# Splitting the first two large experts' weights two turns earlier, and finishing the last large expert in quarters, in a two-layer language-model tower on one core

## The chip, the cores and the metric

One NeuronCore of one Trainium2 chip runs the whole program in one launch. The metric is device time in microseconds (us); lower is better.

## The reference, cut to what matters

A token embedding for 32 batches of 128 tokens (width 192), a causal attention, a soft mixture of 64 small experts, a 12-head attention with rotary positions, and last a routed mixture of 8 large experts:

```python
router_logits = xf @ router_w                       # 4096 tokens x 8 experts
expert_gate  = max(softmax(router_logits)); expert_index = argmax(...)
position_in_expert = cumsum(one_hot(expert_index))  # over all tokens, in order
# a token past the expert's capacity of 512 is dropped
h = gelu(einsum('ecd,edm->ecm', expert_inputs, w1) + b1)      # 192 -> 768
expert_outputs = gelu(einsum('ecm,emd->ecd', h, w2) + b2)     # 768 -> 192
out = einsum('ecd,tec->td', expert_outputs, combine)          # gate times output, back to the token
return h_before + out
```

All of it is in float32. For some products a matrix is split into a high part (written as `fp32r`) and a low part (what that left over), and the products of the parts are summed.

## The kernel before, in words

The program is written engine by engine: in each phase a block gives SP (DMA issue), POOL (GpSimd), PE (TensorE), ACT (ScalarE) and DVE (VectorE) its own list of instructions, and semaphores (`wait_ge`, `then_inc`) order them across engines. An engine runs its list strictly in the order in which it is written. Three phases matter here.

**`combine_phase`** combines the small experts' outputs, computes the second attention, adds it to `h`, and routes. It runs as a software pipeline in turns t = 0 to 37 over 32 batches (`NB`). A turn works on several batches at once: `y` (batch t: combine), `q` (t-1: heads and rotary), `a` (t-2: softmax and values), `p` (t-3: projection, layernorm). Routing goes by pairs of batches: `r` (router logits, from turn 5 on, every second turn), `z` (choice of the expert and counting, one turn later), `w` (row of each token in its expert's table, and the scatter by indirect DMA into `routed_inputs`, one more turn later). At the end the turns are thin: turn 32 has a, p, q and z; turn 33 has a, p, r, w; turn 34 p, z; turn 35 r, w; turn 36 only z of the last pair; turn 37 only w of the last pair. PE is given products that nobody reads (`keep_busy`, L67) in its waits there.

DVE's part of the routing is a chain of small operations: L1797 and L1798 (logits less their maximum), L1834 to L1863 (choice, one-hot, running count, `chosen`), PE's counting product (L1637, recorded as L60), L1804 to L1807 (`read_counts`), L1829 to L1853 (row of the token, `placed`), then POOL's two scatters (L1561).

The first two large experts' w1 are loaded in turn 28 (`load_first_weights`). Their high parts are made by ACT (L1774) at the ends of turns 34 and 35, their low parts by DVE (L1945) at the ends of turns 35 and 36. The second expert's parts lie in the buffers of the small experts' outputs, which turn 31 reads last.

When the last pair's scatters have landed, SP and ACT load the rows of large experts 0 and 1, and the block ends. POOL waits for the scatters too.

**`expert_phase`** with `routed_to` set runs the 8 large experts. For expert n PE makes the hidden layer in six pieces of 128 units (m = 0 to 5; five products each, L60), ACT applies the activation (L1319), PE turns the rows of expert n+2 (L1218), and then makes the output: four groups j of 128 rows, six products of 192 columns each (L1246; the profile has 48 records for the 24 products). The groups lie in two PSUM banks, two groups in each, and are signalled by halves. DVE adds the bias (L1404, a half of 384 columns at a time), ACT applies the activation (`send`, L1304), DVE multiplies by the gate (`gate`, L1409 and L1413), and POOL scatters each group of 128 rows with an accumulating indirect DMA into the output (L1197). `send(n-1)` stands on ACT behind the second hidden piece of expert n; `gate(n-1)` stands on DVE before the bias of expert n; for the last expert (n = 7) both follow at the very end. POOL waits for `gated` before groups 0 and 2, and at the end for `stored`, the landing of all scatters.

Of the kernel before, what the change touches and what calls it, by code (L numbers as in the profile page):

```python
# [21 lines left out]
F32 = mybir.dt.float32  # L22
# [1034 lines left out]
def expert_phase(nc, T, name, L, dst, b2, act_fn, sem_of, routed_to=None, then=None):  # L1057
# [9 lines left out]
    with ExitStack() as ctx:  # L1067
# [41 lines left out]

        def ybank(u):  # L1110

            return bank[:, 4 + 2 * u:6 + 2 * u, 0:2 * D]
# [9 lines left out]
        with nc.Block() as block:  # L1122

            @block.sync
            def _(sp):
# [41 lines left out]
                if then is not None:  # L1167
                    then.sync(sp)

# [16 lines left out]
            if routed:  # L1186

                @block.gpsimd
                def _(pool):
                    def turn(i):  # L1190
                        for u in range(2):
                            n = i * 2 + u

                            for j in range(4):
                                if j % 2 == 0:
                                    wait_apart(pool, gated, 2 * n + j // 2 + 1)
                                pool.indirect_dma_start(  # L1197
                                    out=routed_to,
                                    out_offset=bass.IndirectOffsetOnAxis(ap=numbers[u][:, j, :], axis=0),
                                    in_=ysum[u][:, j, :], in_offset=None, bounds_check=NB * P - 1,  # L1200
                                    oob_is_err=False, compute_op=ALU.add).then_inc(stored[u], 16)

                    each_pair(pool, turn)
                    for u in range(2):
                        pool.wait_ge(stored[u], 64 * turns)

            @block.tensor
            def _(pe):
# [13 lines left out]
                def turn(i):  # L1222
                    for u in range(2):
# [16 lines left out]
                        past(pe, y_added, halves * (n - 1))  # L1240
                        for j in range(4):
                            js = slice(j * P, (j + 1) * P)
                            for k in range(MT):
                                if j == 0:
                                    pe.wait_ge(acted, n * MT + k + 1)
                                last = pe.matmul(ybank(u)[:, j // 2, (j % 2) * D:(j % 2 + 1) * D], hf[:, k, js],  # L1246
                                                 w2s[u][:, k, :], start=k == 0, stop=k == MT - 1)
                            if (j + 1) % (4 // halves) == 0:
                                last.then_inc(w2_done, 1)
# [14 lines left out]
            def _(act):  # L1264
# [32 lines left out]
                def send(n, u):  # L1297

                    if routed:

                        past(act, gated, 2 * (n - 1))
                        for k in range(2):
                            act.wait_ge(y_added, 2 * n + k + 1)
                            act.activation(stage[u][:, 2 * k:2 * k + 2, :], ysum[u][:, 2 * k:2 * k + 2, :], act_fn  # L1304
                                           ).then_inc(act_steps, 1)
# [5 lines left out]
                def turn(i):  # L1311
                    for u in range(2):
                        n = i * 2 + u
                        if not isinstance(n, int) or (2 if routed else 1) <= n + 1 < n_exp:
                            w1_hi(n + 1, 1 - u, i + u)
                        for m in range(MT):
# [4 lines left out]
                            if m == (1 if routed else MT - 1) and (not isinstance(n, int) or n > 0):  # L1321
                                send(n - 1, 1 - u)
                        if routed:
                            load_tags(n, u)
# [20 lines left out]
            def _(dve):  # L1345
# [35 lines left out]
                def turn(i):  # L1381
                    for u in range(2):
# [17 lines left out]
                        y_in = ybank(u).rearrange("p a (c d) -> p a c d", c=2)  # L1400
                        for k in range(halves):
# [17 lines left out]
                if routed:  # L1419
                    gate(n_exp - 1, 1, turns - 1)  # L1420
# [4 lines left out]
def combine_phase(nc, ins, T, out, early, large, sem_of):  # L1425
# [3 lines left out]
    with ExitStack() as ctx:  # L1429
# [78 lines left out]
        with nc.Block() as block:  # L1508
# [34 lines left out]
            def _(pool):  # L1543
# [40 lines left out]
                for k in range(3):  # L1584
                    pool.wait_ge(scattered[k], 32 * ((NPAIR + 2 - k) // 3))
# [128 lines left out]
            def _(act):  # L1714
                def exp_combine(b):
# [5 lines left out]
                def turn(t, u, n, y, q, a, p, r, z, w):  # L1721
# [14 lines left out]
                    if z is not None:  # L1736
                        act.wait_ge(S["logits_read"], z + 1)
                        act.activation(lex[:], lx[:], ACT.Exp).then_inc(S["router_exped"], 1)
                    if a is not None:
# [6 lines left out]
                    if q is not None:  # L1746
                        act.wait_ge(S["qkT_done"], q + 1)
                        past(act, S["S_done"], 4 * q)
                        act.activation(kqT[:], bank[:, 1:3, 0:3 * P], ACT.Copy).then_inc(S["qk_took"], 1)  # L1749
                    if y is not None:  # L1750
# [19 lines left out]
                    if t in (NB + 2, NB + 3):  # L1770

                        k = t - NB - 2
                        act.wait_ge(large.w1_in[k], 48)
                        act.activation(large.w1hi[k][:], large.w1raw[k][:], ACT.Copy).then_inc(large.w1_hi_ready, 1)  # L1774

# [9 lines left out]
            def _(dve):  # L1785
# [15 lines left out]
                def read_counts(z):  # L1801
# [6 lines left out]
                                             ).then_inc(S["counts_read"], 1)  # L1808

# [8 lines left out]
                def turn(t, u, n, y, q, a, p, r, z, w):  # L1818
# [102 lines left out]
                    if p is not None:  # L1921
                        dve.wait_ge(steps, stats5)
                        dve.tensor_scalar(ve[:, 1:2], mv[:, 1, 1:2], EPS, None, ALU.add).then_inc(S["ln5_var"], 1)
                    if z is not None:
                        read_counts(z)
# [15 lines left out]
                    if t in (NB + 3, NB + 4):  # L1941
                        k = t - NB - 3

                        dve.wait_ge(large.w1_hi_ready, k + 1)
                        dve.tensor_tensor(large.w1lo[k][:], large.w1raw[k][:], large.w1hi[k][:].bitcast(F32),  # L1945
                                          ALU.subtract).then_inc(large.w1_split, 1)
# [77 lines left out]
```

## Time and profile before

| what | us |
| --- | --- |
| median of 3 runs | 1408.03 |
| range of the runs | 1406.95 to 1409.55 |
| the profiled execution, its own time | 1409.95 |
| its span, first to last instruction | 1408.2 |
| PE busy | 1332.5 (95%) |
| DVE busy | 971.5 (69%) |
| ACT busy | 936.1 (66%) |
| POOL busy | 253.6 (18%) |
| mean granted TensorE clock | 0.986 |

The span is 1.75 us shorter than the execution's own time. The busy shares say which engine is full on average over phases with different limits; what a change in one stage is worth is read from the chain of waits and from the instructions of that stage in order of time. In the routing's last turns and after the last matmul, PE is mostly idle or runs products that nobody reads.

### The profile page before, as it was taken

The page shows a single profiled execution, that of the slowest core. Times are in us where ns is not written, and L with a number is a line of the kernel's source. Part 1 is how long each engine was busy: PE and PEld are TensorE (multiplying, and loading weights), DVE is VectorE, ACT ScalarE, POOL GpSimd, SP SyncE. Part 2 cuts the span into 40 slices and gives each one's busy share as a digit, 9 for nine tenths or more (in the row PEclk, how much of TensorE's full clock was granted, in tenths as well). Part 3 has the DMA queues.
Part 4 walks back from the last instruction along what each step waited for, and adds up shares of the span by engine and source line. Part 5 has one row for each costly group of instructions (what it writes and reads, how often), then busy time and mean ns, then how long its engine had stood idle before and what let it go on. Part 6 is the DMA issues. An engine that isn't in the chain of part 4 may idle for free. (4 is left out here: it accounts for less than half of the span.)

```text
span 1408.2 us, 29711 instructions
## 1 busy us (share of the span) xinstructions
PE 1332.5 (95%) x9086; PEld 1190.7 (85%) x9086; DVE 971.5 (69%) x2953; ACT 936.1 (66%) x2209; POOL 253.6 (18%) x284
## 2 busy tenths in 40 slices
PE   8799999998999999999999999799999999879995
PEld 6688888886899989998999998688898888768895
DVE  7888877555877777777777773588888888632321
ACT  1488888886666666666666664488888888725551
POOL 5422200001111111111111110012122122111344
PEclk9999999999999999999999999999999999989998
DMA  6144444455666666656665664544454547015631
GB/s 199 45 159 162 162 153 154 157 203 170 196 196 197 186 189 190 200 182 198 190 193 185 193 188 160 160 150 140 154 160 139 152 149 215 15 48 147 158 70 17
DMA packets 181635, 221.04 MB, mean 157 GB/s; under 512 B 25348, under 2 KB 148458, under 8 KB 181536
## 3 DMA queue, kind: packets, MB, share of 16 engines
q1 hardware_dynamic: 147904, 179.52, 41.0%
q10 hardware_dynamic: 25952, 33.32, 7.2%
q0 software_dynamic: 7680, 6.95, 2.7%
q8 instruction: 52, 0.85, 0.3%
q14 instruction: 47, 0.39, 0.1%
HBM read 142.36 MB, written 79.90 MB: 158 GB/s over the span
## 5 line engine op out<-in xcount | busy, mean ns | idle before, releaser
L1246 PE MATMUL bank<-e_w,e_h_full 128*128 128x192 f32 x1920 | 324.7, 326 | 0.4
L1246 PEld LDWEIGHTS bank<-e_w,e_h_full 128*128 128x128 f32 x1920 | 310.6, 190 | 1.7 <-ACT e_h_full L1319 1.3
L1319 ACT ACTIVATE e_h_full<-bank,e_b 128x512 f32<-128x512 f32 x240 | 165.2, 689 | 191.5 <-PE bank L60 191.5
L1180 POOL TENSOR_TENSOR e_ln_rstd<-e_ln_var_eps,minus_half 128x4 f32<-128x4 f32 x62 | 62.5, 1008 | 450.6 <-DVE e_ln_var_eps L1369 450.6
L1727 ACT ACTIVATE probs<-bank,head_neg_max 128x128 f32<-128x128 f32 x384 | 134.9, 393 | 7.6 <-DVE head_neg_max L1823 5.7
L1376 DVE TENSOR_SCALAR e_rows<-e_slot_sums,e_ln_mean_var,e_ln_rstd 128x192 f32<-128x192 f32 x248 | 77.5, 376 | 77.6 <-POOL e_ln_rstd L1180 77.6
L1289 ACT ACTIVATE e_x_full<-bank,e_ln_shift,e_ln_gain 128x512 f32<-128x512 f32 x124 | 89.7, 774 | 44.8 <-PE bank L1218 44.8
L1002 PE MATMUL bank<-x,dispatch_weights 128*128 128x193 f32 x512 | 95.7, 329 | 6.9 <-ACT slot_stage L845 5.9
L60 PE MATMUL bank<-e_x_hi,e_w1hi 128*128 128x512 f32 x216 | 95.4, 442 | 2.3 <-ACT e_h_full L1319 1.2
L1607 PE MATMUL bank<-slot_outputs_then_w_part,combineT 128*128 128x193 f32 x512 | 94.0, 336 | 2.5 <-ACT combineT L1719 2.1
L1404 DVE TENSOR_TENSOR e_stage<-bank,e_b 128x768 f32<-128x768 f32 x64 | 61.3, 957 | 46.5 <-PE bank L1246 46.4
L1607 PEld LDWEIGHTS bank<-slot_outputs_then_w_part,combineT 128*128 128x128 f32 x512 | 84.6, 192 | 9.0 <-issue 9.0
L705 DVE TENSOR_REDUCE column_neg_max<-bank 128x4 f32<-128x512 f32 x64 | 44.2, 690 | 68.5 <-PE bank L60 68.4
L1002 PEld LDWEIGHTS bank<-x,dispatch_weights 128*128 128x128 f32 x512 | 81.9, 190 | 11.0 <-issue 11.0
L1727 ACT ACTIVATION_READ_ACCUMULATOR probs<-bank,head_neg_max 128x1 f32 x384 | 89.2, 232 | 0.0
L823 ACT ACTIVATE slot_exp<-bank,column_neg_max 128x128 f32<-128x128 f32 x256 | 72.9, 373 | 20.2 <-DVE column_neg_max L705 20.2
L60 PE MATMUL bank<-e_x_hi,e_w1lo 128*128 128x512 f32 x216 | 85.3, 395 | 0.0
L60 PE MATMUL bank<-e_x_lo,e_w1hi 128*128 128x512 f32 x216 | 85.2, 394 | 0.0
L60 PE MATMUL bank<-e_x_hi_over_lo,e_w1hi 128*128 128x512 f32 x216 | 85.1, 394 | 0.0
L60 PE MATMUL bank<-e_x_hi_over_lo,e_w1lo 128*128 128x512 f32 x216 | 85.0, 393 | 0.0
L1295 ACT ACTIVATE e_x_hi<-e_x_full 128x1024 fp32r<-128x1024 f32 x70 | 74.0, 1058 | 7.5
L1218 PEld LDWEIGHTS bank<-ident,e_rows 128*128 128x128 f32 x560 | 66.7, 143 | 11.1 <-DMA e_rows<-routed_inputs 1.6
(285 smaller groups left out, 3081.7 us busy)
## 6 DMA issues: line engine op xcount, KB each, us to landing
slot_sums<-slot_stage SPq DMA_DIRECT2D x64, 386.0 KB, 3.2
e_slot_sums<-slot_sums SPq DMA_DIRECT2D x64, 386.0 KB, 3.6
slot_outputs<-e_stage ACTq DMA_DIRECT2D x64, 384.0 KB, 3.2
slot_outputs_then_w_part<-slot_outputs SPq DMA_DIRECT2D x32, 768.0 KB, 4.8
e_w<-in_w SPq DMA_DIRECT2D x64, 288.0 KB, 2.9
slot_logits<-kept_logits SPq DMA_DIRECT2D x32, 512.0 KB, 3.0
slot_logits<-slot_logits SPq DMA_DIRECT2D x32, 512.0 KB, 3.4
e_w1raw<-in_w SPq DMA_DIRECT2D x80, 192.0 KB, 2.7
```

What stands on the lines that cost most here:

```text
L60: last = pe.matmul(out, w, m, start=n == 0, stop=n == len(pairs) - 1, **kw)
L823: last = act.activation(ls[:, n % 2, js], logits_bank(n)[:, js], ACT.Exp, bias=nmc[:, n % 2, j:j + 1])
L1002: last = pe.matmul(U[:, j // 2, j % 2, :], disp[:, n % 2, j * P:(j + 1) * P], x3[n // NC % 3][:, j, 0:1 + D], start=True, stop=True)
L1180: pool.tensor_tensor(rs[u][:], ve[u][:], half[:], ALU.pow).then_inc(rstd_ready, 1)
L1218: last = pe.transpose(bank[:, k, j * P:(j + 1) * P], rows[u][:, j, k * P:(k + 1) * P], ident[:])
L1246: last = pe.matmul(ybank(u)[:, j // 2, (j % 2) * D:(j % 2 + 1) * D], hf[:, k, js], w2s[u][:, k, :], start=k == 0, stop=k == MT - 1)
L1289: last = act.activation(xf[:, k, :], bank[:, k, :], ACT.Identity, bias=lnb[:, k, ds(n, 1)], scale=lng[:, k, ds(n, 1)])
L1295: act.activation(xhi[u][:], xf[:], ACT.Copy).then_inc(x_hi_ready, 1)
L1319: act.activation(hf[:, m, :], hbank(u, m), act_fn, bias=b1s[:, m, ds(n, 1)]).then_inc(acted, 1)
L1376: last = dve.tensor_scalar(rows[u][:, j, 0:D], sums[u][:, j, 1:], mv[u][:, j, 0:1], rs[u][:, j:j + 1], ALU.subtract, ALU.mult)
L1607: last = pe.matmul(bank[:, 0, 0:D + 1], cT[:, c, :], ysb[u][:, c, :], start=c == 0, stop=c == NC - 1)
L1727: last = act.activation(pr[:, s, g, :], bank[:, 4 + s, g * P:(g + 1) * P], ACT.Exp, bias=nmx[:, s, g:g + 1], accum_out=esum[:, s, g:g + 1])
```

## The change

1. ACT's two high parts of the large weights move from turns 34 and 35 into turn 32: the first behind the router's exponential, the second behind the copy of the turned heads.
2. DVE's two low parts move from turns 35 and 36 to the end of turn 32 and into turn 33, ahead of that turn's `read_logits`.
3. The last large expert (`in_quarters`) puts its four output groups into four PSUM banks, one each, and signals each. DVE adds the bias and multiplies by the gate by quarters (192 columns), ACT applies the activation by quarters, POOL waits before each of its four scatters. PE waits before the output until expert 6's bias additions have read their banks.
4. On ACT, the loading of expert 7's tags and the activation of expert 6's output move from behind expert 7's second hidden piece (the tags: its last) to ahead of its first.
5. The final wait for the landing of all scatters moves from POOL to SP, and POOL's wait at the end of `combine_phase` goes.

```diff
@@ expert_phase
+        def in_quarters(n):
+            return routed and isinstance(n, int) and n == n_exp - 1
+        def quarter(j):
+            return bank[:, 4 + j, 0:D]
@@ SP
                 if then is not None:
                     then.sync(sp)
+                if routed:
+                    for u in range(2):
+                        sp.wait_ge(stored[u], 64 * turns)
@@ POOL
                             for j in range(4):
-                                if j % 2 == 0:
+                                if in_quarters(n):
+                                    wait_apart(pool, gated, 2 * n + j + 1)
+                                elif j % 2 == 0:
                                     wait_apart(pool, gated, 2 * n + j // 2 + 1)
...
-                    for u in range(2):
-                        pool.wait_ge(stored[u], 64 * turns)
@@ PE
-                        past(pe, y_added, halves * (n - 1))
+                        past(pe, y_added, halves * (n if in_quarters(n) else n - 1))
...
+                            y = quarter(j) if in_quarters(n) else ybank(u)[:, j // 2, (j % 2) * D:(j % 2 + 1) * D]
...
-                            if (j + 1) % (4 // halves) == 0:
+                            if in_quarters(n) or (j + 1) % (4 // halves) == 0:
                                 last.then_inc(w2_done, 1)
@@ ACT, send
-                        for k in range(2):
+                        parts = 4 if in_quarters(n) else 2
+                        for k in range(parts):
+                            js = slice(k * 4 // parts, (k + 1) * 4 // parts)
                             act.wait_ge(y_added, 2 * n + k + 1)
-                            act.activation(stage[u][:, 2 * k:2 * k + 2, :], ysum[u][:, 2 * k:2 * k + 2, :], act_fn
-                                           ).then_inc(act_steps, 1)
+                            act.activation(stage[u][:, js, :], ysum[u][:, js, :], act_fn).then_inc(act_steps, 1)
@@ ACT, turn
+                        if in_quarters(n):
+                            load_tags(n, u)
+                            send(n - 1, 1 - u)
                         for m in range(MT):
...
@@ DVE, turn
+                        if in_quarters(n):
+                            dve.wait_ge(tags_in[u], 16 * (i + 1))
+                            dve.tensor_copy(numbers[u][:], tags[u][:, :, 1:2])
+                            for j in range(4):
+                                dve.wait_ge(w2_done, 2 * n + j + 1)
+                                dve.tensor_tensor(ysum[u][:, j, :], quarter(j), b2s[u][:], ALU.add
+                                                  ).then_inc(y_added, 1)
+                                dve.wait_ge(act_steps, 2 * n + j + 1)
+                                dve.tensor_scalar(ysum[u][:, j, :], stage[u][:, j, :], tags[u][:, j, 0:1], None, ALU.mult
+                                                  ).then_inc(gated, 1)
+                            continue
@@ combine_phase, POOL
                 each_turn(turn)
-                for k in range(3):
-                    pool.wait_ge(scattered[k], 32 * ((NPAIR + 2 - k) // 3))
@@ combine_phase, ACT, turn
+                    if t == NB:
+                        large_w1_hi(0)
                     if a is not None:
                         for k in range(3):
                             act.wait_ge(S["pT_done"], 3 * a + k + 1)
...
+                    if t == NB:
+                        large_w1_hi(1)
                     if y is not None:
                         act.wait_ge(S["x4T_done"], y + 1)
...
-                    if t in (NB + 2, NB + 3):
-
-                        k = t - NB - 2
-                        act.wait_ge(large.w1_in[k], 48)
-                        act.activation(large.w1hi[k][:], large.w1raw[k][:], ACT.Copy).then_inc(large.w1_hi_ready, 1)
@@ combine_phase, DVE, turn
+                    if t == NB + 1:
+                        large_w1_lo(1)
                     if z is not None:
                         read_counts(z)
...
-                    if t in (NB + 3, NB + 4):
-                        k = t - NB - 3
...
+                    if t == NB:
+                        large_w1_lo(0)
```

Where the pieces stand in the engines' lists. DVE, turns 35 (its end), 36 and 37, before (L1829 is the first operation of turn 37):

```order
L1797 TENSOR_REDUCE router_neg_max<-bank 128x2
L1798 TENSOR_TENSOR router_less_max<-bank,router_neg_max 128x16
L1945 TENSOR_TENSOR e_w1lo<-e_w1raw,e_w1hi 128x1536
L1834 SCALAR_TENSOR_TENSOR ranked<-router_less_max,rank 128x16
L1848 TENSOR_REDUCE first<-ranked 128x2
L1856 TENSOR_TENSOR onehot<-ranked,first 128x16
L1863 TENSOR_TENSOR counted_so_far<-counted_so_far,onehot 128x8
L1804 TENSOR_TENSOR counted_so_far<-counted_so_far,onehot 128x8
L1805 TENSOR_TENSOR over_limit<-bank,expert_limit 128x16
L1807 SCALAR_TENSOR_TENSOR row_by_expert<-over_limit,bank 128x16
L1945 TENSOR_TENSOR e_slot_outputs_then_w_part<-e_w1raw,e_slot_outputs_then_w_part 128x1536
L1829 TENSOR_TENSOR row_by_expert<-row_by_expert,onehot 128x16
```

The same stretch in the changed kernel has both 1536-column operations gone from it. They now stand here, DVE at the end of turn 32 and in turn 33:

```order
L1969 TENSOR_SCALAR x_rows<-h_all,ln_mean_var,ln_rstd 128x192
L1835 TENSOR_TENSOR e_w1lo<-e_w1raw,e_w1hi 128x1536
L1851 TENSOR_REDUCE head_neg_max<-bank 128x6 x2
...
L1951 TENSOR_SCALAR ln_var_eps<-ln_mean_var 128x1
L1835 TENSOR_TENSOR e_slot_outputs_then_w_part<-e_w1raw,e_slot_outputs_then_w_part 128x1536
L1820 TENSOR_REDUCE router_neg_max<-bank 128x2
```

L1969 is L1939 of before, L1851 is L1823, L1951 is L1923, and L1820 is L1797: each low part now stands ahead of an operation that waits for PE.

ACT in the last expert's turn, before:

```order
L1319 ACTIVATE e_h_full<-bank,e_b 128x512 x2
L1304 ACTIVATE e_stage<-e_ysum 128x384 x2
L1319 ACTIVATE e_h_full<-bank,e_b 128x512 x4
L1272 DMA e_tags<-routed_inputs 128x4x2
L1304 ACTIVATE e_stage<-e_ysum 128x384 x2
```

and in the changed kernel:

```order
L1281 DMA e_tags<-routed_inputs 128x4x2
L1315 ACTIVATE e_stage<-e_ysum 128x384 x2
L1332 ACTIVATE e_h_full<-bank,e_b 128x512 x6
L1315 ACTIVATE e_stage<-e_ysum 128x192 x4
```

Expert 6's output activation and the tags' load moved ahead of all six hidden pieces of expert 7, and the last activation is in four pieces.

## Rows read from the trace of the kernel before

**Rows 1.** The page's busy time by engine: busy us (share) xinstructions.
```profile
PE 1332.5 (95%) x9086; PEld 1190.7 (85%) x9086; DVE 971.5 (69%) x2953; ACT 936.1 (66%) x2209; POOL 253.6 (18%) x284
```
**Rows 2.** DVE in order of time, turns 35 to 37: start, us, instruction, [idle before].
```profile
1247.17 0.17 DVE L1798 TENSOR_TENSOR router_less_max<-bank,router_neg_max 128x16 f32<-128x16 f32 x1
1247.26 1.75 DVE L1945 TENSOR_TENSOR e_w1lo<-e_w1raw,e_w1hi 128x1536 fp32r<-128x1536 f32 x1
1248.92 0.17 DVE L1834 SCALAR_TENSOR_TENSOR ranked<-router_less_max,rank 128x16 f32<-128x16 f32 x1
...
1250.94 1.75 DVE L1945 TENSOR_TENSOR slot_outputs_then_w_part<-e_w1raw,slot_outputs_then_w_part 128x1536 fp32r<-128x1536 f32 x1
1252.61 0.17 DVE L1829 TENSOR_TENSOR row_by_expert<-row_by_expert,onehot 128x16 f32<-128x16 f32 x1
```
**Rows 3.** PE in order of time, turn 35 to the first large expert's rows.
```profile
1246.68 1.64 PE L67 MATMUL bank<-spare_operand 128*128 128x512 f32 x6
1249.85 0.46 PE L60 MATMUL bank<-onehot,upto 128*128 128x128 f32 x2 [1.53 <-DVE counted_so_far L1863]
...
1260.69 1.16 PE L67 MATMUL bank<-spare_operand 128*128 128x512 f32 x4 [4.22 <-PEq L1508]
1263.00 1.97 PE L1218 MATMUL bank<-ident,e_rows 128*128 128x128 f32 x8 [1.16 <-DMA e_rows<-routed_inputs]
```
**Rows 4.** ACT in order of time, turns 32 to 34.
```profile
1222.23 0.60 ACT L1744 ACTIVATE probsT<-bank 128x512 f32<-128x512 f32 x1 [1.73 <-PE bank L1644]
...
1227.06 0.39 ACT L1760 ACTIVATE head_invT<-bank 128x256 f32<-128x256 f32 x1 [1.41 <-PE bank L1694]
...
1238.36 1.47 ACT L1774 ACTIVATE e_w1hi<-e_w1raw 128x1536 fp32r<-128x1536 f32 x1
```
**Rows 5.** DVE in order of time, turns 32 to 35.
```profile
1226.78 1.82 DVE L1823 TENSOR_REDUCE head_neg_max<-bank 128x6 f32<-128x768 f32 x2 [4.23 <-PE bank L1686]
...
1237.55 0.17 DVE L1797 TENSOR_REDUCE router_neg_max<-bank 128x2 f32<-128x16 f32 x1 [4.37 <-PE bank L60]
...
1241.97 0.36 DVE L1895 TENSOR_TENSOR h_all<-bank,h_all 128x192 f32<-128x192 f32 x1 [1.29 <-PE bank L60]
...
1243.92 0.38 DVE L1939 TENSOR_SCALAR x_rows<-h_all,ln_mean_var,ln_rstd 128x192 f32<-128x192 f32 x1 [0.30 <-POOL ln_rstd L1552]
```
**Rows 6.** The raw weights' DMAs: durations ns min/median/max, first and last start us.
```profile
L226 SPq DMA_DIRECT2D e_w1raw<-in_w x2: 596/621/646, 1176.6 to 1179.1; - x2
```
**Rows 7.** The chain of waits over the last expert: start, us, what.
```profile
1378.20 7.09 PE bank L60 x30
1385.30 7.81 PE bank L1246 x48
```
**Rows 8.** ACT and DVE in order of time, the last large expert.
```profile
1379.40 0.69 ACT L1319 ACTIVATE e_h_full<-bank,e_b 128x512 f32<-128x512 f32 x1 [8.27 <-PE bank L60]
...
1389.33 0.56 DVE L1404 TENSOR_TENSOR e_ysum<-bank,e_b 128x384 f32<-128x384 f32 x1 [6.61 <-PE bank L1246]
1389.98 0.52 ACT L1304 ACTIVATE e_stage<-e_ysum 128x384 f32<-128x384 f32 x1 [3.96 <-DVE e_ysum L1404]
...
1393.67 1.16 DVE L1413 TENSOR_TENSOR e_ysum<-e_stage,e_tags 128x384 f32<-128x384 f32 x2
```
**Rows 9.** POOL in order of time, turn 36 and the last two experts' scatters.
```profile
1248.05 1.00 POOL L1580 COPY x_rows<-token_numbers 128x2 f32<-128x2 f32 x1
...
1383.08 1.54 POOL L1197 DMA_INDIRECT out<-e_ysum,e_token_numbers  x1 [7.77 <-DVE e_ysum L1413]
...
1395.05 1.54 POOL L1197 DMA_INDIRECT out<-e_ysum,e_token_numbers  x1 [4.86 <-DVE e_ysum L1413]
...
1400.59 1.54 POOL L1197 DMA_INDIRECT out<-e_ysum,e_token_numbers  x1 [0.30 <-issue]
```
**Rows 10.** All scatters of the large experts: durations ns min/median/max, first and last start us.
```profile
L1197 POOL DMA_INDIRECT out<-e_ysum,e_token_numbers x32: 1537/1544/1582, 1289.5 to 1400.6; - x32
```
**Rows 11.** Busy time by stretch: length, then PE, PEld, DVE, ACT, POOL, PEclk, DMA, GB/s.
```profile
1264.00:1268.00 4.00, 4.00 (x17) 3.49 (x15) 1.28 (x2) 2.25 (x3) 0.00 (x0) 0.50 0.45 121
```

More of the change, by code:

```diff
@@ L1245, in turn @@
                                     pe.wait_ge(acted, n * MT + k + 1)
-                                last = pe.matmul(ybank(u)[:, j // 2, (j % 2) * D:(j % 2 + 1) * D], hf[:, k, js],
-                                                 w2s[u][:, k, :], start=k == 0, stop=k == MT - 1)
-                            if (j + 1) % (4 // halves) == 0:
+                                last = pe.matmul(y, hf[:, k, js], w2s[u][:, k, :], start=k == 0, stop=k == MT - 1)
+                            if in_quarters(n) or (j + 1) % (4 // halves) == 0:
                                 last.then_inc(w2_done, 1)
@@ L1320, in turn @@
                                            bias=b1s[:, m, ds(n, 1)]).then_inc(acted, 1)
-                            if m == (1 if routed else MT - 1) and (not isinstance(n, int) or n > 0):
+                            if m == (1 if routed else MT - 1) and not in_quarters(n) and (
+                                    not isinstance(n, int) or n > 0):
                                 send(n - 1, 1 - u)
-                        if routed:
+                        if routed and not in_quarters(n):
                             load_tags(n, u)
@@ L1418, in _ @@
                 each_pair(dve, turn)
-                if routed:
-                    gate(n_exp - 1, 1, turns - 1)
                 if then is not None:
@@ L1714, in _, with large_w1_hi @@
             def _(act):
+                def large_w1_hi(k):
+                    act.wait_ge(large.w1_in[k], 48)
+                    act.activation(large.w1hi[k][:], large.w1raw[k][:], ACT.Copy).then_inc(large.w1_hi_ready, 1)
                 def exp_combine(b):
@@ L1808, in read_counts, with large_w1_lo @@
                                              ).then_inc(S["counts_read"], 1)
+                def large_w1_lo(k):
+                    dve.wait_ge(large.w1_hi_ready, k + 1)
+                    dve.tensor_tensor(large.w1lo[k][:], large.w1raw[k][:], large.w1hi[k][:].bitcast(F32),
+                                      ALU.subtract).then_inc(large.w1_split, 1)
                 def widen():
@@ L1940, in turn @@
                                           ALU.subtract, ALU.mult).then_inc(S["x5_ready"], 1)
-                    if t in (NB + 3, NB + 4):
-                        k = t - NB - 3
-                        dve.wait_ge(large.w1_hi_ready, k + 1)
-                        dve.tensor_tensor(large.w1lo[k][:], large.w1raw[k][:], large.w1hi[k][:].bitcast(F32),
-                                          ALU.subtract).then_inc(large.w1_split, 1)
+                    if t == NB:
+                        large_w1_lo(0)
                 dve.memset(rw0[:], 0.0)
```

## The prediction

> **What bounds the kernel now.** I read the page first: PE is busy 95% of the span, DVE 69%, ACT 66%, POOL 18% [rows 1]. That average says nothing of the two places that the change touches, so I followed the chain of waits to them and then read each engine there in order of time.
>
> The first place is the routing of the last pair of batches (turns 35 to 37). Nothing is left beside it, so each step of that one chain is on the path: logits, choice, count, row, scatter, load of expert 0's rows, and all eight large experts after that. Two operations lie in the chain that don't belong to it: the low parts of the weights, 1.75 us each on DVE [rows 2]. The logits less their maximum end at 1247.34, and the choice, which needs only them, starts at 1248.92. The counts' reading ends 0.08 us behind the second low part's start, as L1798 does behind the first's, so at 1251.02, and the row operation that needs only the counts starts at 1252.61. PE meanwhile idles 1.53 us for the choice [rows 3].
>
> The second place is what follows the last matmul. PE's last output products run from 1385.30 to 1393.11 [rows 7]. POOL's first scatter of the last expert starts at 1395.05 and the fourth at 1400.59, so one every 1.85 us, each 1.54 us long [rows 9]. The end of the program is then bound by POOL, with every other engine idle. Those four could start one by one while PE still works, if the rows were handed over as they come.
>
> **The change part by part.**
>
> *Low parts out of turns 35 and 36.* The choice can start 0.03 us behind L1798: 1247.37 instead of 1248.92, 1.55 us earlier. The row operation can start at 1251.05 instead of 1252.61, 1.56 us. Between the two stands PE's counting product, which may be held by PE's own list. Its six unread products start at 1246.68 [rows 3]. They take 1.64 us by the modelled end, 1248.32, though the array can take the next product some 0.15 us before such an end. The choice would be in at about 1248.16 and the count product at 0.14 us behind it (1249.71 to 1249.85 before), 1248.30. So PE is free in the same moment, and I count 0 for this, with up to 0.15 us lost. **Term: -3.1 us**, and everything that follows (scatter, barrier, rows) moves with it. POOL's copy in turn 36 also gets its usual length back: it lasted 1.00 us [rows 9] and ended as the low part on DVE ended. It isn't on the path.
>
> *Where the four operations go.* ACT has 1.73 us idle before L1744 in turn 32, and a high part takes 1.47 us: it fits with 0.26 us left [rows 4]. The second has 1.41 us before L1760, so it overshoots by 0.06 us at most. Behind L1760 stand one more copy and then the exponentials, which wait for DVE's maximum (of 1226.78 to 1228.6, the first half at 1227.7 [rows 5]); so the overshoot costs 0 to 0.1 us, and I take 0. DVE has 4.23 us idle ahead of L1823 and 4.37 us ahead of L1797 for 1.75 us each [rows 5]: both fit with over 2 us left. What is behind the low part of turn 33 is L1797, which waits for PE's router product at 1237.5 anyway. The raw weights were asked for by 1179.1, 40 us ahead [rows 6], so the waits for them are met. POOL's reciprocal root in turn 33 falls together with the low part; if it is held as the copy was, it is about 1.7 us late, and its reader comes only behind L1797, some 4 us later. **Term: 0**, at most +0.1. If the cover were gone entirely, 2 x 1.47 + 2 x 1.75 = 6.4 us would show.
>
> *POOL's wait at the end of the routing.* SP and ACT wait for the same scatters and then still issue four loads, so POOL was not last at the barrier. Rows 3 show PE back at 1260.69, and it then waits 1.16 us for the rows. Term: 0.
>
> *The last expert.* The 48 products are even, so the quarters are ready at about 1387.3, 1389.3, 1391.2 and 1393.1. Each quarter then goes through DVE's addition, ACT's activation, DVE's product. For 192 columns: addition out of PSUM 0.36 (L1895 [rows 5]), activation between 0.27 (0.69 for 512 columns and 0.52 for 384 [rows 8], carried on in a straight line) and 0.52, I take 0.30, near the line, product 0.38 (L1939 [rows 5]), and two hand-overs of 0.03 to 0.09 (1389.89 to 1389.98 [rows 8]), 0.12 together. Sum 1.16 us. So the last quarter is gated at 1393.13 + 1.16 = 1394.29. Before, the first half was gated at 1393.67 + 0.56 = 1394.23 (L1413 takes what the equally wide addition takes) and POOL started 0.82 us behind it. The same gap puts the last scatter at 1395.1 instead of 1400.59. It would be bound by PE plus 2 us of hand-over, not by POOL: quarters come every 1.95 us and POOL needs 1.85. **Term: -5.5 us.**
>
> This holds only if POOL is free at the first quarter, gated at about 1388.5 and due on POOL at 1389.3. Before, POOL had expert 6's four scatters from 1383.08 on, to 1390.2: 0.9 us too late, and with 1.85 us a piece it would only slowly catch up. This is what the moved activation is for. Expert 6's last product ends at 1378.2 [rows 7] and its second addition takes 0.56, so until 1378.8; ACT is idle for 8.27 us until 1379.40 [rows 8], and a 384-column activation takes 0.52: done at 1379.4, in time for the hidden piece. DVE's gate then follows at about 1379.3 and POOL starts at 1380.1 instead of 1383.08, done by 1387.3. Cover for the activation: that idle time; if it ends 0.1 us late, the hidden piece is 0.1 us late, and PE has two hidden banks, so nothing shows. The tags' load, 0.5 us on ACT's queue, moves into the same idle time. PE's wait for expert 6's additions is met 6 us early.
>
> *The last wait on SP instead of POOL.* 1400.59 to the span's end is 7.6 us: scatter, landing, barrier, clearing, barrier. The scatter and landing stay. I bound the move of the wait by -0.5 and +0.5 us, a hand-over or two either way, and take 0.
>
> DVE's operations now run beside POOL's descriptor making. The row that bears on it is POOL's copy of 1.00 us beside a DVE operation of 1.75 us [rows 9, 2]: POOL can be held. All 32 scatters before took 1.54 to 1.58 us, most of them beside DVE work of some kind [rows 10]. The Trainium skill, SBUF — State Buffer, Who interferes with whom, says that a two-input DVE operation holds only POOL's reads, while a `tensor_scalar` from SBUF to SBUF can take both ports and keep POOL from writing descriptors. The change turns the gate's product from the former into the latter. By that rule a quarter could hold POOL for its 0.38 us; it is a rival below.
>
> **Sum:** -3.1 - 5.5 = -8.6 us. Against the profiled execution's 1409.95 that is 1401.35; that execution is 1.9 us above the median of the runs shown, and against the median, 1408.03, it is **1399.4 us**.
>
> **The rivals.**
>
> *R1, POOL's pace binds the last scatters.* The margins are thin: POOL's previous scatter ends at 1393.1 + 1.54 and needs 0.30 more, so it is free 0.1 to 0.2 us before the last quarter is due. If each of DVE's products holds POOL for 0.38 us, the pace becomes 2.23 us, and three of them from 1389.3 give 1396.0, 0.9 us later than forecast: 1400.3. For: the 1.00 us copy. Against: no scatter of the 32 was over 1.58 us [rows 10]. Chance 0.12. That by the same rule the product would be faster is worth under 0.1 us.
>
> *R2, the clock comes out otherwise.* PE was granted 0.50 (1.2 GHz) between 1264 and 1268 [rows 11], behind an idle time of 4.22 us, and the eight turns of expert 0's rows took 1.97 us [rows 3]. PE's unread products now end about 1.6 us earlier and the rest comes 3.1 us earlier, so this idle time shrinks to some 2.7 us. If PE stays at 2.4 GHz, the turns take half, 1.0 us less: 1398.4. If instead the clock rises at the same moment as before, it is 3.1 us later in the work, and half of that is lost on the first hidden products: +1.6, 1401.0. Chance 0.12 each way.
>
> *R3, only one of the two low parts was worth anything.* PE's unread products or the barrier absorb the other, 1.55 us: 1401.0. Chance 0.07. If the moved operations weren't hidden at all, +6.4: 1405.8, which isn't told from no change. Chance 0.03.
>
> *R4, slower.* The half clock stays through expert 0. PE is then the bound, and a stretch at 1.2 GHz costs half its length. An expert takes 15 us (7.09 and 7.81 [rows 7], and the turns). To give back 8.6 us the half clock would have to last 17 us longer, and 23 us to be clearly slower; through experts 0 and 1 (some 31 us) it would cost 15.5 us: 1414.9. Against: it lasted under 7 us before. Chance 0.02.
>
> **How the numbers follow.** The forecast has 0.52, R1 0.12, R2 0.24 (both ways), R3 0.10, R4 0.02. A measurement of this kernel can tell about 0.2% (2.8 us) from no change. The forecast, R1, R2 and R3's first case are all faster by more: 0.95. R3's second case is within: 0.03. R4 is slower: 0.02. The range takes in R2 below, with the unknown of the last wait (0.5) and some of the runs' own spread (1.1 us below the median), 1396.9, and above R1, R2 and R3's first case with the same, 1402.4.
>
> **What would show it.** Right: no 1536-column operation on DVE between the logits and the scatter, the choice 0.03 us behind L1798; the last scatter about 3.1 us nearer to the router's last product; head_neg_max of turn 33 at the same time as before; POOL's scatters of expert 6 starting 3 us nearer to that expert's end; four quarter scatters about 1.95 us apart, the last 2 us behind PE's last product. Wrong: scatters longer than 1.6 us or 2.2 us apart (R1); first turns of expert 0 at 1.0 us, or slow hidden products (R2); idle time of PE before the counting product as long as before (R3).

## The result, and the profile after

The changed kernel took 1400.53 us (median of 5 runs, 1397.76 to 1403.23) against 1409.55 us for the kernel before on the same chip (median of 5, 1406.95 to 1411.06). The ratio is 0.9932, with an interval of 0.9919 to 0.9946: 9.6 us faster, 7.6 to 11.4. The forecast was 1399.4 us in a range of 1396.9 to 1402.4, and 8.6 us faster.

The page of the profiled execution (its own time 1397.76 us), first lines:

```profile
span 1395.8 us, 29717 instructions
...
PE 1329.0 (95%) x9086; PEld 1187.3 (85%) x9086; DVE 972.8 (70%) x2957; ACT 936.8 (67%) x2211; POOL 254.6 (18%) x284
```

Busy times are those of [rows 1], within 4 us. What changed is where the engines wait. The two spans differ by 12.4 us, and part of that isn't the change: turn 33's `head_neg_max`, which comes before anything that was taken off the path, is already 2.15 us earlier (1224.63 against 1226.78). The same instruction starts anywhere from 1224.63 to 1230.04 in the fourteen traces of this document (both kernels and twelve runs). So I go by distances inside the trace.

DVE in order of time, the end of the routing (start, us, instruction, [idle before]), answers to [rows 2]:

```profile
1244.87 0.17 DVE L1821 TENSOR_TENSOR router_less_max<-bank,router_neg_max 128x16 f32<-128x16 f32 x1
1245.08 0.26 DVE L1862 SCALAR_TENSOR_TENSOR ranked<-router_less_max,rank 128x16 f32<-128x16 f32 x1
...
1247.10 0.17 DVE L1830 SCALAR_TENSOR_TENSOR row_by_expert<-over_limit,bank 128x16 f32<-128x16 f32 x1
1247.38 0.17 DVE L1857 TENSOR_TENSOR row_by_expert<-row_by_expert,onehot 128x16 f32<-128x16 f32 x1
```

Both gaps are closed to 0.04 and 0.11 us. PE over the same stretch, as [rows 3]:

```profile
1243.46 1.16 PE L60 MATMUL bank<-router,x5T 128*128 128x128 f32 x8 [0.69 <-ACT x5T L1759]
1244.38 1.64 PE L67 MATMUL bank<-spare_operand 128*128 128x512 f32 x6
1246.10 0.46 PE L60 MATMUL bank<-onehot,upto 128*128 128x128 f32 x2
...
1254.58 1.17 PE L67 MATMUL bank<-spare_operand 128*128 128x512 f32 x4 [1.86 <-PEq L1531]
1257.69 1.97 PE L1227 MATMUL bank<-ident,e_rows 128*128 128x128 f32 x8 [1.94 <-DMA e_rows<-routed_inputs]
```

The counting product has no idle time before it any more. From the last router product to the scatter of the last 128 tokens it was 1255.41 - 1245.76 = 9.65 us before and is 1250.17 - 1243.46 = 6.71 now: **2.94 us** less. The eight turns of expert 0's rows still take 1.97 us.

The moved operations, ACT and POOL in order of time, turns 32 and 33, against [rows 4]:

```profile
1218.20 1.55 ACT L1738 ACTIVATE e_w1hi<-e_w1raw 128x1536 fp32r<-128x1536 f32 x1
1220.42 0.60 ACT L1771 ACTIVATE probsT<-bank 128x512 f32<-128x512 f32 x1 [0.68 <-PE bank L1665]
...
1223.40 1.48 ACT L1738 ACTIVATE slot_outputs_then_w_part<-e_w1raw 128x1536 fp32r<-128x1536 f32 x1
1224.91 0.38 ACT L1789 ACTIVATE head_invT<-bank 128x256 f32<-128x256 f32 x1
```

```profile
1231.12 2.01 POOL L1575 TENSOR_TENSOR ln_rstd<-ln_var_eps,minus_half 128x1 f32<-128x1 f32 x1 [0.70 <-DVE ln_var_eps L1951]
```

They are hidden: from turn 32's `head_neg_max` to turn 33's it is 11.65 us, and was 11.67. POOL's reciprocal root lasts 2.01 us instead of some 0.55, beside the low part on DVE (1230.95, 1.75 us), and nobody waits for it.

POOL over the last two experts, against [rows 9], and then the chain behind the last quarter:

```profile
1374.85 1.54 POOL L1208 DMA_INDIRECT out<-e_ysum,e_token_numbers  x1 [4.83 <-DVE e_ysum L1438]
...
1383.82 1.54 POOL L1208 DMA_INDIRECT out<-e_ysum,e_token_numbers  x1 [1.85 <-DVE e_ysum L1423]
1385.75 1.54 POOL L1208 DMA_INDIRECT out<-e_ysum,e_token_numbers  x1 [0.39 <-issue]
1387.68 1.54 POOL L1208 DMA_INDIRECT out<-e_ysum,e_token_numbers  x1 [0.39 <-issue]
1389.61 1.54 POOL L1208 DMA_INDIRECT out<-e_ysum,e_token_numbers  x1 [0.39 <-issue]
```

```profile
1387.67 0.36 DVE L1420 TENSOR_TENSOR e_ysum<-bank,e_b 128x192 f32<-128x192 f32 x1 [0.82 <-PE bank L1256]
1388.46 0.32 DVE L1423 TENSOR_SCALAR e_ysum<-e_stage,e_tags 128x192 f32<-128x192 f32 x1 [0.43 <-ACT e_stage L1315]
```

The addition starts with PE's last product done. From there to the last scatter's start it was 7.46 us (1400.59 - 1393.13) and is 1.94: **5.52 us** less. The last quarter is gated at 1388.78 and POOL starts 0.83 us behind it.

One more distance changed that I hadn't counted. From the last scatter's start to the end of the span it was 1408.2 - 1400.59 = 7.61 us, and is 1395.8 - 1389.61 = 6.19: **1.42 us** less. The engines' own queues show why; first the block's end before, then after (count, duration ns min/median/max, first and last start):

```profile
L1122 POOLq DRAIN  x2: 1120/1892/2665, 843.5 to 1404.1; - x2
L1122 POOLq COMPARE_BRANCH  x1: 41/41/41, 1404.0 to 1404.0; - x1
```

```profile
L1128 POOLq DRAIN  x2: 1122/3042/4961, 842.8 to 1389.4; - x2
L1128 SPq COMPARE_BRANCH  x1: 38/38/38, 1393.1 to 1393.1; - x1
```

Two blocks end at this line, so each queue has two drains; the later and longer one of POOL's is the one at the kernel's end. The branch stands behind the wait for the landing and shows when that wait was met. At a block's end POOL drains. Before, it first waited for the landing (until 1404.0) and then drained for 2.67 us, up to 1406.8, with all engines waiting at the barrier. Now the drain begins at 1389.4, behind the issue of the last scatter, and lasts until 1394.4, beside the landing that SP sees at 1393.1.

The three distances sum to 9.9 us; the runs' ratio says 9.6. The rest of the 12.4 us between the spans is the 2.15 us from before turn 33 and three stretches of 0.07 to 0.15 us: from `head_neg_max` of turn 33 to the last router product (18.98, now 18.83), from the last scatter of the routing to expert 0's rows (7.59, now 7.52) and from there to the last addition (130.13, now 129.98).

### The profile page after: what moved, and what is told of

The parts are those of the page before. It is cut to its first block and busy times, and to the rows that moved or that the text cites. A ratio compares the mean times of both kernels' runs of the same rounds, so it can differ in the third digit from the quotient of the medians.

```text
span 1395.8 us, 29717 instructions
## 1 busy us (share of the span) xinstructions
PE 1329.0 (95%) x9086; PEld 1187.3 (85%) x9086; DVE 972.8 (70%) x2957; ACT 936.8 (67%) x2211; POOL 254.6 (18%) x284
```

## Experiments

The runs of one kernel spread by 2 to 4.5 us either way (1402.8 to 1411.7 in the twelve runs of `a_route_only`), so the runs' ratios can't tell differences of 1 us from each other. The verdicts on single terms come from distances in the traces. Where the work is the same, the one from the last router product to the last scatter and the one from the last addition to the last scatter repeat to 0.04 us; the one from there to the end repeats to 0.25 us. All ratios are to the kernel before on the same chip.

**The routing part alone** (`a_route_only`): the kernel before with the diff of `combine_phase`, and POOL's wait kept.

> The kernel before with the routing part alone: the four weight-splitting operations in turns 32 and 33, both of POOL's waits kept. If the two low parts were each in the chain: the time from the last router product to the turn of expert 0's rows falls from 17.24 us to 14.2, and the whole is 3.0 us faster. If only one counted (the rival), 15.7 us and 1.5 us faster.

Measured: ratio 0.9975 (0.9962 to 0.9989), 3.5 us faster. From the last router product to the last scatter 6.70 us. To the turn of the rows it was 14.81 and not 14.2: the load of expert 0's rows took 5.28 us against 4.67 in the changed kernel. That load varies by half a microsecond from execution to execution (4.75, 4.80, 4.85, 5.14 in four others), so the distance to the scatter is the one to read. Both low parts counted.

**The quarters alone** (`a_quarters_only`): the kernel before with the diff of `expert_phase`, POOL's last wait kept.

> The kernel before with the last expert's quarters and the moved activation alone, both of POOL's waits kept. My sum: the last scatter starts 1.96 us behind PE's last product instead of 7.48, and the whole is 5.5 us faster. If the last wait's place is what gave the 1.4 us at the end, the time from the last scatter's start to the end of the span stays at 7.6 us.

Measured: ratio 0.9962 (0.9949 to 0.9976), 5.4 us faster. Last scatter 1.93 us behind the start of the last addition, 7.70 us from there to the end. Both as expected.

**The last wait alone** (`a_last_wait_sp`):

```diff
@@ the kernel before, SP
                 if then is not None:
                     then.sync(sp)
+                if routed:
+                    for u in range(2):
+                        sp.wait_ge(stored[u], 64 * turns)
@@ POOL
                     each_pair(pool, turn)
-                    for u in range(2):
-                        pool.wait_ge(stored[u], 64 * turns)
```

> The kernel before with only the last wait for the scatters' landing moved from POOL to SP. Theory of the drain: POOL drains at the end of its block, 2.67 us that came behind the landing and now runs beside it, so the time from the last scatter's start to the end of the span falls from 7.6 to 6.2 us and the whole by 1.4 us (0.1%). Rival: the shorter end comes from the quarters (fewer bytes or descriptors in flight at the end); then it stays 7.6 us.

Measured: 6.04 us from the last scatter to the end of the span, with the rest of that end unchanged (7.46 us from the last addition to the last scatter). Ratio 0.9991 (0.9978 to 1.0004): the runs alone couldn't have shown it, the trace does. By the runs' ratios the three parts alone give 3.5, 5.4 and 1.3 us, in sum 10.2, against 9.6 for the changed kernel. The queues of this kernel:

```profile
L1122 POOLq DRAIN  x2: 1120/4926/8733, 844.5 to 1395.4; - x2
```

The longer of the two drains is the one at the end. It begins at 1395.4, with three scatters still to start, and ends at 1404.1; SP sees the landing at 1403.0.

**The changed kernel with both of POOL's waits back** (`a_after_pool_waits`).

> The changed kernel with both of POOL's waits as before. Theory of the drain: 1.4 us slower than the changed kernel, all of it between the last scatter's start and the end (7.6 us); the barrier behind the routing takes 3.1 us again instead of 2.3, and PE still waits for the rows behind it, so that costs 0. Rival: the earlier barrier matters too, 0.9 us more.

Measured: 7.77 us at the end, drain of 2.67 us from 1398.5. Behind the routing PE came back 3.1 us behind the landing of the scatters (1257.01 to 1260.14), 2.3 in the changed kernel (1252.32 to 1254.58), and in both it then waited for the rows. Ratio 0.9934 (0.9916 to 0.9952), not distinguishable from the changed kernel's by the runs. So of POOL's two waits the last is worth 1.4 to 1.6 us and the one behind the routing nothing. All traces agree on the last one: with POOL waiting it is 7.52 to 7.77 us from the last scatter's start to the end (four kernels), with SP or ACT waiting 6.04 to 6.23 (ten).

**Expert 6's activation back in its place** (`b_send_late`):

```diff
@@ the changed kernel, ACT
                         if in_quarters(n):
                             load_tags(n, u)
-                            send(n - 1, 1 - u)
...
-                            if m == (1 if routed else MT - 1) and not in_quarters(n) and (
+                            if m == (1 if routed else MT - 1) and (
                                     not isinstance(n, int) or n > 0):
```

> The changed kernel with expert 6's output activation back behind expert 7's second hidden piece (the tags stay early). My reason for the move was that POOL must be free: expert 6's four scatters then start about 3 us later, end at about 0.5 us behind the time at which the first quarter is due, and since POOL needs 1.85 to 1.93 us a scatter and the quarters come every 1.95, the delay is carried to the last: last scatter 2.7 to 2.9 us behind PE's last product instead of 1.94, 0.8 to 1.0 us slower. Rival: the quarters catch up or the move didn't matter, 1.94 us as before.

Measured: the last scatter starts 2.92 us behind the start of the last addition instead of 1.94, 1.0 us more. POOL in order of time:

```profile
1389.38 1.55 POOL L1208 DMA_INDIRECT out<-e_ysum,e_token_numbers  x1 [0.30 <-DVE e_ysum L1422]
1391.24 1.54 POOL L1208 DMA_INDIRECT out<-e_ysum,e_token_numbers  x1 [0.30 <-DVE e_ysum L1422]
...
1396.79 1.54 POOL L1208 DMA_INDIRECT out<-e_ysum,e_token_numbers  x1 [0.30 <-issue]
```

Eight scatters run back to back here, 1.85 us apart, and the delay of the first reaches the last. The quarters come every 1.95 us, so only 0.1 us a scatter is won back. Ratio 0.9935 (0.9917 to 0.9954).

**The second low part alone back in turn 36** (`b_lo1_back`):

```diff
@@ the changed kernel, DVE
-                    if t == NB + 1:
-                        large_w1_lo(1)
...
                     if t == NB:
                         large_w1_lo(0)
+                    if t == NB + 4:
+                        large_w1_lo(1)
```

> The changed kernel with the second low part alone back at the end of turn 36. If each low part was in the chain by itself: from the router's last product to the second scatter 8.2 us (6.71 + 1.5), 1.5 us slower. Rival (one of the two is absorbed by PE's unread products): 6.7 us, no change.

Measured: 8.18 us from the last router product to the last scatter, so 1.47 us for this low part; the other 1.47 is the first's. Each stood in the chain by itself. Ratio 0.9931 (0.991 to 0.9952): 1.5 us is again below what the runs tell.

**The gate's product with two inputs** (`d_gate_tt`): in the quarters `tensor_tensor` with the gate broadcast, where the change has `tensor_scalar`.

> The changed kernel with the gate's product of the quarters as a two-input operation (the gate broadcast) instead of one with a scalar per row. If the one-input form took both ports and held POOL, POOL's scatters would be shorter or start sooner behind their gate here; since they took 1.54 us beside it, I expect no change: 1.54 us, last scatter 1.94 us behind PE's last product, same time. If the one-input form was quicker because of both ports, the product now takes longer than 0.32 to 0.36 us.

Measured: scatters of 1.54 us, last scatter 1.97 us behind the last addition, product 0.36 us instead of 0.32 to 0.36. Ratio 0.9938 (0.9916 to 0.996). No effect of the form on POOL.

**The last wait on ACT** (`d_last_wait_act`), where the change has it on SP.

> The changed kernel with the last wait for the scatters' landing on ACT instead of SP. Theory of the drain: what counts is only that POOL doesn't hold it, so its drain runs beside the landing as on SP: 6.1 to 6.2 us from the last scatter's start to the end, and the same time. Rival: SP itself is quick at a block's end and ACT isn't; then 6.5 us or more (ACT's own drain took 0.4 to 1.4 us).

Measured: 6.09 us from the last scatter to the end. ACT's drain behind its wait took 0.008 us, POOL's 4.86, begun before the landing. Ratio 0.9928 (0.9909 to 0.9947). It isn't SP that is quick; it is POOL that must not be the one who waits.

**The changed kernel again** (`d_after_again`).

> The changed kernel again, unaltered, as the yardstick for the three beside it: 0.993 of the kernel before, last scatter 1.94 us behind PE's last product, 6.2 us from its start to the end of the span.

Measured: ratio 0.9937 (0.9918 to 0.9956), median 1401.47; 1.93 and 6.16 us.

The last three experiments are about the clock, a rival of the prediction, and led to a faster version.

**More unread products ahead of expert 0's rows** (`b_warm`): `keep_busy(pe, T, idle_bank, 12)` for 4.

> The changed kernel with 12 unread products instead of 4 ahead of the first rows of expert 0. If PE's idle time there is what sets the clock to 1.2 GHz for the first turns (1.97 us for eight), they now run at 2.4 GHz in most executions: 0.9 to 1.0 us for eight, and the whole 1.0 to 1.5 us faster. Rival: the idle time at the barrier (1.86 us) is enough to let the clock fall, the turns stay 1.97 us and nothing changes.

Measured: neither theory came out whole. The rival was right that the clock falls behind the idle time at the barrier, but the turns changed all the same. One stretch with its granted clock (0.65, the column before the DMA share), then PE in order of time:

```profile
1258.75:1263.00 4.25, 4.24 (x13) 3.25 (x14) 0.00 (x0) 1.49 (x2) 0.00 (x0) 0.65 0.90 241
```

```profile
1258.76 4.40 PE L67 MATMUL bank<-spare_operand 128*128 128x512 f32 x12 [1.90 <-PEq L1531]
1262.96 1.26 PE L1227 MATMUL bank<-ident,e_rows 128*128 128x128 f32 x8
```

The clock fell behind the barrier all the same (0.65 is a mean of the two levels), the twelve products ran mostly at 1.2 GHz and took 4.4 us where at 2.4 GHz it would be some 3.0 (an estimate from 1.64 us for six and 6.18 us for 26 of them), and the rows had to wait for them: 15.32 us from the router product to the turns instead of 14.2 to 14.7. The turns then took 1.26 us. The turns gained 0.7 us and the wait lost 0.6 to 1.1; ratio 0.9932 (0.9915 to 0.995). The Trainium skill, TensorE: Matmul & The Clock Gate, Wait — 56ns, not 53.3ns?, gives 215.7 ns from start to start of a 512-column product at the full clock and 426.7 at the half one. An estimate from these figures for 12 products is 2.6 and 5.1 us, and the 4.4 measured lie between.

**Unread products in turns 32 and 33** (`c_warm_turns`), into idle times of PE that the change had left:

```diff
@@ the changed kernel, PE, behind the projection
                                 ).then_inc(S["p_done"], 1)
+                    if t in (NB, NB + 1):
+                        pe.wait_ge(S["v_took"], t - 1)
+                        keep_busy(pe, T, bank[:, 3, :], 7)
```

> The changed kernel with 7 unread products each in turns 32 and 33, in PE's idle times of 2.1 us before the exponentials are done. In the profile of the changed kernel PE ran at 1.2 GHz behind each of them (twelve transposes 2.6 us instead of 1.4), on the chain. If the idle times are the cause: the clock stays at 2.4 GHz, the time from turn 33's head_neg_max to the last router product falls from 18.8 us to 16.5, with up to 1.7 us more in turn 32; 2 to 3.5 us faster (0.15 to 0.25%). Rival: the chain is bound by ACT and DVE there and the unread products only stand in the way, 0 to 1 us slower.

**and four more ahead of turn 33's projection** (`d_warm_more`):

```diff
+                        if t == NB + 1:
+                            pe.wait_ge(S["v_took"], NB)
+                            keep_busy(pe, T, bank[:, 3, :], 4)
                         pe.wait_ge(S["o_ready"], p + 1)
```

> The kernel with unread products in turns 32 and 33, and 4 more in turn 33's idle time of 1.3 us ahead of the projection, behind which the clock still fell. If idle time is what lets it fall, PE stays at 2.4 GHz through turns 32 to 35 and the time from turn 33's head_neg_max to the router's last product falls from 17.2 to 16.5 us, 0.991 to 0.990 of the kernel before. Rival: the four stand in the projection's way: 17.3 us or more.

Measured: ratios 0.9903 (0.9884 to 0.9922) and 0.9902 (0.9882 to 0.9922), so the runs don't tell these two apart. On the same chip `d_warm_more` took 1396.50 us, the changed kernel 1401.47 and the kernel before 1409.64. It beats both. Against the changed kernel it is 5.0 us in the medians, and no run of the one reaches the other's (1394.44 to 1398.48 against 1399.76 to 1402.74, six each); the traces agree on where it comes from. PE in turn 33, first in the changed kernel, then in `d_warm_more`:

```profile
1229.98 1.12 PE L1650 MATMUL bank<-ident,x_rows 128*128 128x128 f32 x4 [2.06 <-ACT probs L1752]
1230.89 2.77 PE L1665 MATMUL bank<-ident,probs 128*128 128x128 f32 x12
1233.45 1.92 PE L60 MATMUL bank<-router,x5T 128*128 128x128 f32 x8
```

```profile
1229.47 1.90 PE L67 MATMUL bank<-spare_operand 128*128 128x512 f32 x7
1231.82 0.66 PE L1656 MATMUL bank<-ident,x_rows 128*128 128x128 f32 x4 [0.45 <-issue]
1232.31 1.47 PE L1671 MATMUL bank<-ident,probs 128*128 128x128 f32 x12
1233.62 1.06 PE L60 MATMUL bank<-router,x5T 128*128 128x128 f32 x8
```

And the granted clock over such stretches, in the same order:

```profile
1231.00:1235.00 4.00, 4.00 (x21) 4.00 (x20) 1.70 (x2) 2.39 (x4) 2.01 (x1) 0.50 0.02 6
```

```profile
1232.00:1236.00 4.00, 4.00 (x41) 3.56 (x43) 3.15 (x11) 2.55 (x6) 2.27 (x2) 1.00 0.02 6
```

In the changed kernel PE idles 2.06 us for the exponentials and then does the transposes, which everybody waits for, at 1.2 GHz. With its idle time filled, it does them at 2.4 GHz: 1.47 us for twelve instead of 2.77. From turn 32's `head_neg_max` to turn 33's it is 10.05 us instead of 11.65, and from there to the last router product 16.20 instead of 18.83 (17.15 in `c_warm_turns`, where 7 products ran at half clock behind the idle time of 1.34 us and took 3.09 us). Sum 4.2 us against this trace of the changed kernel. The twelve traces without these products vary themselves, though: 11.16 to 11.67 and 17.53 to 19.06 us, together 29.20 to 30.71 against 26.25, so the gain is 3.0 to 4.5 us.

Which idle time lets the clock fall isn't settled for turn 33. There are two, 1.34 us ahead of the projection and 2.06 us behind it. In the changed kernel the clock fell inside the second. In `c_warm_turns`, which fills only the second, it fell just behind the first, as PE took up the projection. Only `d_warm_more`, which fills both, kept it at 2.4 GHz through the turn.

## Why the prediction was right, point by point

- **Low parts out of turns 35 and 36, forecast -3.1, measured -2.94.** Right; the difference is in the 0.11 us between the counts and the row operation, where 0.03 had been taken, and in the choice operation itself (0.26 us instead of 0.17). PE's unread products neither helped nor hindered, as counted. R3, that only one of the two was worth anything, is refuted by the run with the second one back (1.47 us).
- **The four operations hidden, forecast 0, measured 0** (11.65 us against 11.67 between the two maxima). POOL's root was held, 2.01 us, as foreseen from the copy.
- **The last expert, forecast -5.5, measured -5.52.** The sizes inside it: addition 0.36 (0.36), activation 0.36 (0.30 taken), product 0.32 to 0.36 (0.38). The reason given for the moved activation holds: without it 1.0 us is lost, where 0.9 had been worked out for POOL's lateness.
- **POOL's wait behind the routing, forecast 0, measured 0.** The barrier got 0.9 us quicker (3.1 us behind the landing of the scatters, now 2.3) and the rows hid it.
- **The last wait on SP, forecast 0 in bounds of -0.5 to +0.5, measured -1.4.** This is the step that was mis-sized. I took the 7.6 us behind the last scatter for landing and barriers and asked only which engine wakes sooner. In it were 2.67 us of POOL's drain, of which 1.4 can run beside the landing. The page doesn't show drains as busy time; the queue's own rows for the block's last line do. The sum came out 1.3 us short of what the traces show, and the time still 1.1 us above the forecast, because the median of before was 1409.55 in this measurement and not 1408.03. That the forecast lies so near is partly luck: the drain's 1.4 us and the 1.5 us between the two medians point opposite ways. The mechanisms of the two large terms are what was foreseen.
- **R1, POOL's pace.** Refuted: 1.54 us for every scatter. The spacing of 1.93 us is the quarters' own; each starts 0.82 to 0.83 us behind its gate. The margin was thin all the same, 0.39 us idle of which 0.30 is always there. The Trainium skill, SBUF — State Buffer, Who interferes with whom, says that a `tensor_scalar` can take the port pair that DVE shares with POOL, when its operands let it run in a two-port mode, and so hold POOL's descriptor making. Neither the scatters beside it nor the run with the other form show that at 192 columns. The same section's other rule, that a DVE operation with two inputs in SBUF holds a POOL operation that reads SBUF, agrees with the root's 2.01 us beside the low part.
- **R2, the clock.** It came out as before in the profile: 1.97 us for the first turns, half clock for 6.5 us. PE's idle time at the barrier, foreseen at some 2.7 us, was 1.86, since the barrier came 0.9 us sooner; the clock fell behind it even so. What it does elsewhere can be seen in turns 33 to 35: from turn 33's `head_neg_max` to the last router product, where the work is the same, the traces without unread products there have between 17.53 and 19.06 us.
- **R4, slower.** Nothing of it.

## What to carry to other kernels

Read each step of a tail or a hand-off chain for work that doesn't belong to it, and take it out to where its engine waits for another anyway: the gain is then nearly its full length (here 1.47 us for each operation of 1.75). When an engine's queue has several pieces of fixed length behind the last computation, hand them over as they come, and check that the queue is free when the first arrives, since a late start is carried to the last. Let the final wait for transfers stand on an engine whose drain is short, and not on the one that issued indirect DMAs.

## What the runs showed of the hardware that I had not expected

- POOL's drain at the end of a block takes 2.67 us when it starts behind the landing of its indirect DMAs (2665 ns in four kernels, and 2678 ns at the end of the routing before), and SP's and ACT's 0.01 to 0.4 us there. Started earlier it takes 4.6 to 8.7 us, but ends 1.1 to 1.5 us behind the landing.
- PE's idle times of 2.1 us in turns 32 and 33 went with 3 to 7 us at 1.2 GHz each (the kernel before, the changed one twice, `a_route_only`, `b_warm`). With unread products in them and in the 1.3 us ahead of turn 33's projection, the two turns up to the last router product took 3.0 to 4.5 us less. In `c_warm_turns` the clock fell right behind an idle time of only 1.34 us.
